# A four-layer attention and spectral kernel on one core: one projection for the scores of layer 1, layer 3 over half the positions, group norms folded into weights, and new orders on every engine

## What is computed

```python
# layer 0: attention over 2x2-pooled keys, heads of 16 and 64 channels
theta, phi, g = x@w_theta + b, maxpool(x@w_phi + b), maxpool(x@w_g + b)
x = x + sigma * (softmax(theta @ phi.T) @ g @ w_o + b_o)

# layer 1: group norm (32 groups), one attention head of 128 channels
n = (x - mean) * rsqrt(var + 1e-6) * gamma + beta
q, k, v = n@wq + bq, n@wk + bk, n@wv + bv
x = softmax(q @ k.T / sqrt(128)) @ v @ wo + bo + x

# layer 2: group norm (16 groups), 8 heads of 16 channels
n = (x - mean) * rsqrt(var + 1e-5) * scale + bias
q, k, v = split(n @ w_qkv)
x = softmax(q @ k.T / 4) @ v @ w_out + b_out + x

# layer 3: 2-d Hartley transform over w and c, block-diagonal MLP on z and on
# its mirror image zn = roll(flip(z, (h, w)), 1), soft threshold, transform back
z, zn = dht(x), roll(flip(dht(x), (1, 2)), (1, 1), (1, 2))
o1k = relu(0.5 * (z @ w1a + zn @ w1b) + b1[0])
o1n = relu(0.5 * (zn @ w1a + z @ w1b) + b1[1])
# w1a = w1[0] + w1[1], w1b = w1[0] - w1[1]; o2k, o2n likewise from o1k, o1n
x = dht(softshrink(o2k + o2n)) / (W * C) + x
```

## Time and profile before

| | us |
|---|---|
| median of three runs | 173.66 |
| lowest, highest | 173.12, 174.29 |
| the profiled execution | 173.37 |
| its span | 171.5 |
| PE busy | 164.8 (96%) |
| DVE busy | 109.1 (64%) |
| ACT busy | 109.4 (64%) |
| POOL busy | 27.5 (16%) |
| chain that ended last: PE, DMA, DVE, ACT | 83%, 4%, 4%, 3% |

### The profile page before, as it was taken

One profiled execution on the slowest core, in us unless ns is written; L12 is line 12 of the kernel. 1 busy time (PEld: TensorE's weight loads), 2 busy tenths in 40 slices (PEclk: granted clock), 3 DMA queues, 4 the chain that ended last, 5 costly groups with the idle time before them and its releaser, 6 DMA issues.

```text
span 171.5 us, 3846 instructions
## 1 busy us (share of the span) xinstructions
PE 164.8 (96%) x1473; PEld 124.0 (72%) x1473; DVE 109.1 (64%) x293; ACT 109.4 (64%) x251; POOL 27.5 (16%) x56
## 2 busy tenths in 40 slices
PE   7999979999999999999999999999999999999992
PEld 4687869887767777686888776677857675657881
DVE  1368899899977886837967634979175566123032
ACT  0467568686565788385467877374867856874660
POOL 8011714232122111120011210000011000000100
PEclk9999999999999999999999999999999999999999
DMA  5992000000000000000001001000010000200003
GB/s 139 303 325 108 4 2 2 0 4 0 2 2 4 0 4 6 0 6 0 0 4 34 2 0 36 0 6 2 2 36 2 4 2 2 64 3 6 0 0 92
DMA packets 6353, 5.17 MB, mean 30 GB/s; under 512 B 576, under 2 KB 5952, under 8 KB 6336
## 3 DMA queue, kind: packets, MB, share of 16 engines
q1 hardware_dynamic: 6336, 4.93, 9.5%
HBM read 3.75 MB, written 1.05 MB: 28 GB/s over the span
## 4 chain that ended last, share of the span: by engine, by line
PE 83%; DMA 4%; DVE 4%; ACT 3%; SPq 2%; issue 1%; POOL 0%; DVEq 0%; POOLq 0%
PE psum L537 10%; PE psum L517 9%; PE psum L548 9%; PE psum L445 4%; PE psum L465 4%; DMA x0T<-in_xT 3%; PE psum L599 3%; PE psum L425 2%; PE psum L559 2%; PE psum L455 2%; ACT pT L779 2%; PE psum L618 2%; PE psum L600 2%; PE psum L610 2%; PE psum L575 2%; PE psum L589 2%
## 5 line engine op out<-in xcount | busy, mean ns | idle before, releaser
L984 DVE TENSOR_REDUCE nmax<-psum 128x4 f32<-128x1024 f32 x32 | 38.1, 1216 | 9.1 <-PE psum L517 8.9
L779 ACT ACTIVATE pT<-psum 128x1024 f32<-128x1024 f32 x32 | 32.1, 1022 | 9.3 <-PE psum L537 9.3
L537 PE MATMUL psum<-qk 17*128 17x256 f32 (+1 forms) x256 | 18.3, 400 | 0.2 <-DMA qk<-stage_all 0.2
L517 PE MATMUL psum<-qk 16*128 16x256 f32 (+1 forms) x256 | 18.3, 400 | 0.0
L548 PE MATMUL psum<-pT,vaug_all 128*32 128x256 f32 x256 | 16.5, 384 | 0.0
L517 PEld LDWEIGHTS psum<-qk 16*128 16x128 f32 (+1 forms) x256 | 11.6, 184 | 4.9 <-issue 1.8
L537 PEld LDWEIGHTS psum<-qk 17*128 17x128 f32 (+1 forms) x256 | 11.6, 184 | 4.1 <-ACT oT L784 0.8
L311 POOL TENSOR_TENSOR rstd<-vare,half 128x1 f32<-128x1 f32 x16 | 8.9, 564 | 31.9 <-DVE vare L936 31.8
L548 PEld LDWEIGHTS psum<-pT,vaug_all 128*32 128x32 f32 x256 | 7.1, 109 | 6.0 <-issue 2.3
L316 POOL COPY zE<-zE 128x17 f32<-128x17 f32 x8 | 1.6, 200 | 52.6 <-ACT zE L792 52.6
L784 ACT COPY oT<-psum 128x256 f32<-128x256 f32 x16 | 6.0, 373 | 5.9 <-PE psum L548 5.8
(11 more groups left out here) (137 smaller groups left out, 360.1 us busy)
## 6 DMA issues: line engine op xcount, KB each, us to landing
x0T<-in_xT SPq DMA_DIRECT2D x8, 128.0 KB, 4.9
xin<-in_x SPq DMA_DIRECT2D x8, 128.0 KB, 5.0
out<-x SPq DMA_DIRECT2D x8, 128.0 KB, 2.0
tab<-in_weights SPq DMA_DIRECT2D x1, 580.0 KB, 5.3
qk<-stage_all SPq DMA_DIRECT2D x32, 4.0 KB
tab<-in_weights SPq DMA_DIRECT2D x1, 448.0 KB, 5.4
tab<-in_weights SPq DMA_DIRECT2D x1, 384.0 KB, 5.7
tab<-in_weights SPq DMA_DIRECT2D x1, 200.0 KB, 2.5
```

The source lines that it names most:

```text
L517: last = mm(bank[(b0, b1)[j // 2] + j % 2][:, u * TOK:(u + 1) * TOK], at[:, u, 0, :], at[:, :, 1, :], start=True, stop=True)
L537: last = mm(bank[(b0, b1)[j // 2] + j % 2][:, m * TOK:(m + 1) * TOK], at[:, m, 1, :], at[:, :, 0, :], start=True, stop=True)
L779: go(pT[g](i)[:, 2 * k:2 * k + 2].rearrange("p j m t -> p j (m t)"), pair(home["st", g, i][k]), ACT.Exp).then_inc(s["exp" + "EO"[g]], 1)
L984: v.tensor_reduce(nmax2[g](i)[:, :, 2 * k:2 * k + 2], pair(home["sm", g, i][k]).rearrange("p j (u m) -> p u j m", u=TILES), AX.X, ALU.max, ...
```

## The change

In layer 1 the scores need q and k only as a product, so the new kernel multiplies the two weight matrices once (`w1qk`) and projects each image once (`qk1` has one product; `s1` multiplies the result with the normalised image). A 129th column of `v1m` gives the part of the bias that depends on the position (`e1`), which `score_shift` on DVE adds to the maximum (`nb1`). The group norms' scale and shift go into weights and biases: `group_scale` and `group_shift` go, and `normalised` subtracts the mean and multiplies. For this the opening has new folds: `fold_biases`, `bias_sums`, `bias_wide`, a longer `fold_values` and `values_folded`, `scaled2` (three scaled matrices on POOL), `fold_biases2`, `bias_sums2`, `bias_wide2`, `fold_out2`, `out2_folded`.

In layer 3 the mirror image lets the first MLP product be split into an even and an odd part, each over 9 of 16 rows: POOL adds `zE` and its mirror (`z_sum`), DVE subtracts them (`z_difference`), `am` has two products of 144 columns, ACT copies the odd part (`odd_out`), DVE adds and subtracts it (`a_out`), and `o1k_out` and `o1n_out` take their positions from the result; the second is stored in the order in which `ym` and a mirrored `cas_w` want it, so `om` is two products of 128 columns.

```diff
-    (("mean1", P), ("w1_q", C), ("w1_k", C), ("w1_vT", C), ("w1_o", C), ("bv_wide", C), ("bo_wide", C)),
+    (("mean1", P), ("w1_q", C), ("w1_k", C), ("w1_v", C), ("w1_qT", C), ("w1_kT", C), ("w1_vT", C), ("w1_o", C), ("bo_wide", C)),
...
-    (("mlp", 6 * P), ("cas_c", C), ("cas_w", P), ("cas_we", P // W * WE)),
+    (("mlp", 6 * P), ("cas_c", C), ("cas_w", 2 * P), ("cas_we", P // W * WE)),
...
+            def z_sum(i):
+                pool.wait_ge(s["zE"], i + 1)
+                gp.tensor_tensor(zsum(i), zE(i)[:, 0:HALF, 0:W], zE(i)[:, H:H - HALF:-1, W:0:-1], ALU.add
+                                 ).then_inc(s["zsum"], 1)
+
+            def bias_wide():
+
+                pool.wait_ge(s["b_rd"], 1)
+                gp.tensor_copy(bv_wide[:, :], bqkv[:, 2:3].to_broadcast((P, P)))
+                gp.tensor_copy(bq_wide[:, :], bqkv[:, 0:1].to_broadcast((P, P))).then_inc(s["wide_b"], 1)
+
+            def scaled2(n):
+
+                if n == 0:
+                    pool.wait_ge(s["tab2"], 16)
+                gp.tensor_scalar(w2n[:, n, :], w(("w2_q", "w2_k", "w2_v")[n]), col("L2_conv_gn_scale"),
+                                 (float(HD) ** -0.5, 1.0, 1.0)[n], ALU.mult, ALU.mult).then_inc(s["w2n"], 1)
+
+            def bias_wide2():
+                pool.wait_ge(s["b2_rd"], 1)
+                gp.tensor_copy(bv2_wide[:, :], bv2[:, :].to_broadcast((P, P))).then_inc(s["wide_b2"], 1)
...
+            bias_wide(); scaled2(0); scaled2(1); scaled2(2); bias_wide2(); x1b_out(0); x1b_out(1); mlp_sums()
...
+            def fold_biases(b, *marks):
+
+                freed(*marks)
+                home["fold_biases"] = b
+                pe.wait_ge(s["tab0"], 16)
+                pe.wait_ge(s["tab1"], 16)
+                for n, name in enumerate(("w1_q", "w1_k", "w1_v")):
+                    last = mm(bank[b][:, n:n + 1], w(name), col("L1_conv_gn_beta"), start=True, stop=True)
+                last.then_inc(s["fold_b"], 1)
...
+            def fold_out2(b, *marks):
+                freed(*marks)
+                home["fold_out2"] = b
+                pe.wait_ge(s["wide_b2"], 1)
+                mm(bank[b][:, 0:C], bv2_wide[:, :], w("w2_o"), start=True, stop=True).then_inc(s["fold_o2"], 1)
...
-                mm(bank[b][:, 0:TOK], w("w1_q"), xn[0](i), start=True, stop=True)
-                mm(bank[b][:, TOK:2 * TOK], w("w1_k"), xn[0](i), start=True, stop=True).then_inc(s["qk1"], 1)
...
+                mm(bank[b][:, 0:TOK], w1qk[:, :], xn[0](i), start=True, stop=True).then_inc(s["qk1"], 1)
...
-                mm(both, fold1[:, 0, :], zE(i), start=True, stop=False)
-                mm(both, fold1[:, 1, :], zE(i)[:, ::-1, ::-1], start=False, stop=True).then_inc(s["a"], 1)
+                pe.wait_ge(s["zsum"], i + 1)
+                mm(bank[b][:, 0:HALF * W], fold1[:, 0, :], zsum(i).rearrange("p h w -> p (h w)"), start=True, stop=True)
+                pe.wait_ge(s["zdif"], i + 1)
+                mm(bank[b][:, HALF * W:2 * HALF * W], fold1[:, 1, :], zdif(i).rearrange("p h w -> p (h w)"),
+                   start=True, stop=True).then_inc(s["a"], 1)
...
+            def odd_out(i):
+                act.wait_ge(s["a"], i + 1)
+                copy(odd(i), bank[home["am", i]][:, HALF * W:2 * HALF * W]).then_inc(s["odd"], 1)
...
-            def group_scale(i, layer):
+            def normalised(i, layer):
+
                 dve.wait_ge(s[f"rstd{layer}"], i + 1)
...
+                v.tensor_scalar(xn[k](i), xT_sb[k](i), bank[home[f"gm{layer}", i]][:, 0:1], rstd[k](i), ALU.subtract, ALU.mult
...
+            def z_difference(i):
+                dve.wait_ge(s["zE"], i + 1)
+                v.tensor_tensor(zdif(i), zE(i)[:, 0:HALF, 0:W], zE(i)[:, H:H - HALF:-1, W:0:-1], ALU.subtract
+                                ).then_inc(s["zdif"], 1)
+
+            def a_out(i):
+                dve.wait_ge(s["odd"], i + 1)
+                even = bank[home["am", i]][:, 0:HALF * W]
+                v.tensor_tensor(a2(i)[:, 0:HALF * W], even, odd(i), ALU.add)
+                v.tensor_tensor(a2(i)[:, HALF * W:2 * HALF * W], even, odd(i), ALU.subtract).then_inc(s["aneg"], 1)
```

More of the change, by code:

```diff
@@ L327, in _ @@
+            wrap(6); z_sum(6); wrap(7); z_sum(7)
         @block.tensor
@@ L353, in fold_mlp @@
                 pe.wait_ge(s["mlp_ab"], 1)
[L354 to L355 removed]
+                for m in range(2):
+                    mm(bank[b0][:, m * P:(m + 1) * P], w("cas_c"), mlp_half[:, m, 0:P], start=True, stop=True)
                 for m, blkT in enumerate((mlp_a, mlp_b)):
@@ L625, in om @@
                 pe.wait_ge(s["s3"], i + 1)
-                mm(bank[b][:, 0:TOK], w("cas_w"), s3(i).rearrange("p u c -> p (u c)"), start=True, stop=True
-                   ).then_inc(s["out_ps"], 1)
+                for u in range(TILES):
+                    last = mm(bank[b][:, u * C:(u + 1) * C], w("cas_w")[:, u * P:(u + 1) * P], s3(i)[:, u, :],
+                              start=True, stop=True)
+                last.then_inc(s["out_ps"], 1)
             pe.wait_ge(s["filled"], 1)
-            keep_clock(11, 7); proj0(0, 0); keep_clock(8, 7); proj0(1, 1); s0(0, 0); gwm(0, 2); keep_clock(4, 7)
@@ L631, in _ @@
-            proj0(2, 3); gwm(1, 4); p0t(0, 0); fold_values(5); keep_clock(2, 7); o0(0, 0); s0(1, 1)
-            proj0(3, 5, ("vo_rd", 1)); s0(2, 3); x1t(0, 0); proj0(4, 4, ("gw", 2)); proj0(5, 2)
-            proj0(6, 0, ("xT1", 1)); p0t(1, 1); gm1(0, 5, ("theta", 4)); proj0(7, 6); o0(1, 1); p0t(2, 3); s0(3, 7)
-            gwm(2, 3, ("p0T", 3)); gwm(3, 4); qk1(0, 5); o0(2, 4, ("gw", 4)); x1t(1, 1); v1m(0, 3); s1(0, 5)
-            fold_mlp(3, 1, ("v1", 1)); gm1(1, 7, ("p0", 4)); x1t(2, 4); p1t(0, 5); p0t(3, 4, ("xT1", 3)); o0(3, 4)
@@ new lines, in _ @@
+            keep_clock(2, 7); proj0(2, 4); s0(1, 1); gwm(1, 5); keep_clock(2, 7); p0t(0, 0); fold_values(3); o0(0, 0)
+            gwm(2, 2); fold_biases2(5, ("gw", 2)); p0t(1, 1); proj0(3, 4); s0(2, 6); o0(1, 1)
+            proj0(4, 5, ("b2_rd", 1)); fold_out2(7); proj0(5, 3); proj0(6, 4, ("theta", 4)); x1t(0, 0)
+            proj0(7, 6, ("p0", 3)); x1t(1, 1); p0t(2, 0, ("xT1", 1)); keep_clock(8, 2); gwm(3, 5, ("theta", 5))
+            s0(3, 1, ("xT1", 2)); o0(2, 0); keep_clock(4, 2); gm1(0, 5, ("gw", 4)); fold_mlp(7, 3, ("theta", 6))
@@ new lines, in _ @@
+            gm1(1, 2); x1t(2, 0); qk1(0, 5); v1m(0, 0, ("xT1", 3)); gwm(4, 4, ("theta", 7)); qk1(1, 2); s1(0, 5)
+            v1m(1, 0, ("v1", 1)); s1(1, 7, ("fold1_rd", 1), ("c_rd", 1)); p0t(3, 0, ("v1", 2)); s0(4, 1)
+            keep_clock(1, 3); o0(3, 0); keep_clock(2, 4); p1t(0, 5); gm1(2, 4); keep_clock(1, 3); p1t(1, 7); o1(0, 5)
+            s0(5, 1, ("p0", 5)); o1(1, 0, ("x1", 4)); qk1(2, 4); x1t(3, 6, ("theta", 8)); x2t(0, 5)
+            v1m(2, 1, ("p0", 6)); s1(2, 4); x2t(1, 0); p0t(4, 5, ("xT2", 1)); s0(6, 1, ("v1", 3)); p0t(5, 6)
@@ new lines, in _ @@
+            gwm(5, 0, ("xT2", 2)); gwm(6, 5, ("p0T", 5)); o0(4, 7); gm2(0, 6, ("p0T", 6)); o0(5, 0)
+            gwm(7, 5, ("gw", 7)); s0(7, 3); keep_clock(1, 2); p1t(2, 4); gm2(1, 5, ("gw", 8)); gm1(3, 2); v2m(0, 6)
+            qk2(0, 1, ("p0", 7)); o1(2, 6, ("vaug", 1)); qk2(1, 7); sm(0, 1, 0, 4, ("x1", 6)); v2m(1, 2)
+            x2t(2, 3, ("p0", 8)); qk1(3, 6); v1m(3, 7, ("qkO", 2)); x1t(4, 2, ("vaug", 2)); x1t(5, 3, ("xT2", 3))
+            p0t(6, 0, ("nmaxO", 1)); p0t(7, 1); nt(0, 1, 6, ("q1", 4)); s1(3, 4); keep_clock(2, 5)
@@ L963, in nmax1_out, with score_shift @@
                                 negate=True).then_inc(s["nmax1"], 1)
+            def score_shift(i):
+                dve.wait_ge(s["nmax1"], i + 1)
+                dve.wait_ge(s["v1"], i + 1)
+                for u in range(TILES):
+                    e = e1(i)[:, u:u + 1]
+                    last = v.scalar_tensor_tensor(out=nb1(i)[:, u:u + 1], in0=nmax1(i)[:, u:u + 1], scalar=e, in1=e,
+                                                  op0=ALU.subtract, op1=ALU.add)
+                last.then_inc(s["nb1"], 1)
             def inv1_out(i):
@@ L1064 @@
+            xo(7)
 def kernel(**inputs):
```

411 lines of the change are left out of this document (210 added, 201 removed).

## The result

The changed kernel takes 171.21 us (median of 4 runs, 170.92 to 171.94), the kernel before 173.39 beside it: a ratio of 0.9889 (95% interval 0.986 to 0.9919). A second measurement, on another chip, gave 171.42 against 173.16, ratio 0.991 (0.9892 to 0.9928). So it is 1.0% faster; the forecast was 175.0, 0.8% slower than the 173.66 of the kernel before, with "no change" as the likeliest outcome. The profiled execution took 171.5 us, its span is 169.7.

The account below looks back on a forecast made before the run. The prediction took PE's work to bound the kernel, except in the opening and tail. From 173.4 us, -5.8 + 1.7 + 1.3 + 0.4 = -2.4 gave 171.0; a 4.0 us GpSimd stall made 175.0, range 171.2 to 176.8.

Parts of the forecast that it names:

- PE's work: All images and the new folds: smaller products less added fold products change PE's own work by -5.8 us, fillers apart.
- Other engines: DVE gains 0.4 us per image, +3 on 109 us busy; ACT gains nothing; PE's work covers both.
- The fillers, +1.7: Behind `proj0(2)`: 36 fillers instead of 20, the 16 more priced at 0.109 us each, +1.7 us.
- The middle, +0: Mid-kernel: layer 3's relay of about 2.6 us is covered by 2.7 to 5 us of other PE work; nothing charged.
- The tail, +1.3: From `pv(7,1)` to the last addition: 0.3 us longer where work alone promised 1.0 less, so +1.3 us.
- The opening, +0.4: Table 1 grows by 128 KB ahead of image 2, so `proj0(2)` starts at 9.3 instead of 8.90: +0.4 us.
- The step on GpSimd, +4.0: Opening: code set-up at GpSimd's `ISA` row loses its cover and stalls PE at `fold_out2`, +4.0 us.
- L: Assumed length of GpSimd's set-up in the opening: 6.4 us, five times ScalarE's 1.28 us load, within bounds 0 and 7.8.
- rival A: Opening: GpSimd's set-up is short or runs ahead, so no stall, 171.0 us; chance 0.20.
- The port, 0.4 us per image: Layer 3: DVE's difference and GpSimd's sum, released together, make one wait about 0.4 us per image; covered in the middle.
- Rival B: Behind the opening's stall on PE the clock falls to the lower level, +1.7 us: 176.7 us; chance 0.10.
- Rival C: Middle: `a_out` stands behind maxima, PE reaches `ym` too early, 0.5 us in five images, +2.5: 177.5 us; chance 0.10.

Follow-up runs that it names:

- l3_old: Changed kernel with layer 3 put back to two products of 289 columns, without the relay, in the new orders: 174.6 us.
- both_old: Changed kernel with layer 3 as in l3_old and a second product of 256 columns put back in each layer 1 projection: 177.8 us.
- pool_first: Changed kernel with one unused sum of 128 columns on GpSimd directly behind its memsets: 171.7 us.
- pool_busy3: Changed kernel with three unused sums of 1152 columns on GpSimd between bias_wide and the first scaling of w2n: 175.9 us.

## Why the prediction was wrong

**The bound.** Right: PE at 95%, 87% of the chain.

**PE's work.** Right. The forecast was -5.8 us and +1.7 for the fillers, -4.1; the busy time fell by 3.8. In the chain the second product of `am` shows 0.24 us for 144 columns, as taken.

**Other engines.** DVE's busy time grows by 0.7 us, not 3, and ACT's by 2.0, not nothing. PE is still the bound.

**The fillers, +1.7.** Wrong in the price. They make busy time, but each takes 0.02 us off or on the time, not 0.109; 16 more of them are +0.3. The forecast read the 96% as a share of work, while the 20 fillers of the kernel before stand in waits as well.

**The middle, +0.** Wrong: 2.4 us more of idle at 40 to 160. The forecast compared the relay of layer 3 with its cover, and there it was right (`l3_old`, without the relay, shows the same waits). But it took PE's share of 98 to 100% in the old orders as proof that the new ones would have no waits either, and never went through them for the exponentials and maxima of layer 2. `both_old` shows that nearly all of the new waits come with the new kernel even when PE has its old work. This and the fillers nearly cancel, so that the sum before the last step, 171.0, came out within 0.5 us of the result in part by luck.

**The tail, +1.3.** Right in length: 15.2 us against the forecast of 15.3, with steps between that come up to 0.7 us earlier than listed (`ym(7)` at +10.5 instead of +11.2). The share of the relay was set too high: `l3_old` makes it about 0.6 us, by medians.

**The opening, +0.4.** Nearly: `proj0(2)` starts at 9.49, not 9.3. Copies on GpSimd are 0.29 us (0.5 assumed), `fold_out2` is reached at 15.18 (14.95). Without a set-up the scalings end at 11.86 and one copy of 0.29 follows, so the cover was 3.0 us, not 2.45.

**The step on GpSimd, +4.0.** This is the step that failed, at its first half: "I take five times this, L = 6.4, an estimate inside the bounds". Neither the number five nor the row it was multiplied with said anything about GpSimd. L is under 0.3 us: 0.24 us in the changed kernel, which a transfer accounts for, and 0.08 in `pool_first`. The bounds 0 and 7.8 were right, and with nothing in the trace between them the low end, which made rival A, should have had the larger chance: the mechanism of A is what the runs show, and its 171.0 is near the result, with the luck named above. The Trainium skill, GPSIMD Engine Reference, section 2.1 Instruction dispatch, gives a load of about 6 us for the first call to a freshly loaded kernel; this trace doesn't show it for the first tensor operation of a program that follows the row, neither at 4.60 us in `pool_first` nor at 10.75. The second half, that a stall there goes through to the end, was right (`pool_busy3`), and the lower clock behind it made it longer.

**The port, 0.4 us per image.** Too much. With `z_difference` beside it `z_sum` takes 0.53 to 0.62 us, alone 0.49 (timeline of the changed kernel, images 3 and 6):

```profile
130.04 0.49 POOL L337 TENSOR_TENSOR zsum<-zE 128x144 f32<-128x144 f32 x1
...
158.02 0.31 DVE L1101 TENSOR_TENSOR zdif<-zE 128x144 f32<-128x144 f32 x1 [0.65 <-POOL zE L333]
158.06 0.61 POOL L337 TENSOR_TENSOR zsum<-zE 128x144 f32<-128x144 f32 x1
```

The difference takes 0.30 alone and 0.31 here. In the five images in which DVE's difference starts first, by 0.04 us, GpSimd's sum takes about 0.1 us longer and the difference nothing. In the one in which the sum starts first (73.73 against 73.83), the difference takes 0.60 and the sum 0.53.

**Rival B** (the clock) has its mechanism shown in `pool_busy3`, without its cause in the changed kernel. **Rival C** had the right size of trouble and even its sign (38.26 and 38.87 of 40 us busy), but another cause: 2.4 us in the middle, from layer 2's exponentials and maxima and not from `a_out`.
